# Attention in an AdaLN layer: key-block weights added by VectorE and GpSimd ahead of the product with ones

## The chip, the cores and the metric

One core of a Trainium2 chip runs the whole layer in one launch. The time is device microseconds of one execution; three executions of the kernel before took 2218.84, 2220.32 and 2224.95 us, a median of 2220.32 us. Lower is better.

## The reference

The input is four sequences of 1024 rows by 512 columns, all in float32. A modulated layer norm is followed by causal attention with 16 heads of 32 columns (its queries and keys are projected, rotated and normalised per head), a projection with a gate and a residual, and a gated feed-forward part. What the change touches is this line pair:

```
w = jax.nn.softmax(scores, axis=-1)          # causal, over the keys
a = jnp.einsum('bhqk,bhkd->bhqd', w, v)
```

The softmax's division is done at the end: the kernel computes, for every query, the sum of the exponentials times v and the sum of the exponentials alone, and divides the first by the second.

## The kernel before

The program has four stages: the projections to q, k and v (to about 367 us of the span), attention (to about 1010 us), the output projection, and the feed-forward part (from about 1140 us). The change is in the attention stage, `attention_stage`, alone.

**Groups and blocks.** The 16 x 4 head-and-sequence pairs are handled in 16 groups `n` of four heads `j`. In a group the queries come in four quarters `q` of 256, and the keys in slabs `g` of 256 (two key tiles of 128, `e` = 0 and 1). `BLOCKS` lists the ten causal (q, g) pairs: block 0 is (0,0), 1 (1,0), 2 (1,1), 3 (2,0), 4 (2,1), 5 (2,2), 6 (3,0), 7 (3,1), 8 (3,2), 9 (3,3). Blocks 0, 2, 5 and 9 are `DIAGONAL`; the other six are full ("full steps" in the change's short name).

**One block.** `shift` (TensorE) forms the transposed scores less the row maximum in PSUM, `exponent` (ScalarE) writes their exponentials for the four heads into `probT`, a ring of three buffers, `cut` (GpSimd) zeroes the triangle of diagonal blocks, and `weigh` (TensorE) runs twice: with `summing` false it multiplies with v, eight matmuls of 32 columns of weights; with `summing` true it multiplies with a matrix of ones, to get the sums. The four heads lie on different column groups of the array. Of a full block the sum may be taken after its two key tiles were added: `pair` adds `prob[:, :, 0:256]` and `prob[:, :, 256:512]` in two instructions of two heads each into one of the two buffers `pairs`, and then `weigh` needs only four matmuls with ones in place of eight. Before the change this is done for blocks 1, 3, 4, 6 and 8 (`PAIRED`): by VectorE for 3, 6 and 8 (`BY_VECTOR`), by GpSimd for 1 and 4. Block 7 is not paired.

**Other work in the same loop.** `score` (TensorE) forms the plain scores of a later group in two PSUM slots `psA`, `peak` (VectorE) takes their maxima (a reduce at L1104, a masked one at L1109); `gather` ends a group's maxima with four small operations, `turn_peaks` (TensorE, L1014) transposes them, `copy_peaks` (ScalarE) takes them out. `prepare` (TensorE, L993) transposes q or k of the next group into the same two slots, `widen` (ScalarE), `high` (GpSimd) and `low` (VectorE, L792) go on from there. Slots are handed on in the order of `turns`: whoever takes one waits (`slot_free`) until the user before the last has been read. `normalise` (GpSimd, L970) multiplies a finished group with the inverted sums, which come back by DMA (`wide_in`, L926).

**The order.** Every engine runs through the same written-out list of `STEPS`, and does its part for position k in program order. Within position k = 10 n + r, called turn r here: TensorE does two heads' `shift`, the `score` items of block position r, two heads' `shift`, `weigh` with v, `prepare` if r is 1 or 3, `turn_peaks` if r is 0, and `weigh` with ones. The shifts belong to block r - 2 of an earlier group, the two `weigh` to block r - 3 (both modulo 10). VectorE does `pair` for block r - 3 first, then the `peak` items, then `gather` in turn 9, then `low` in turns 2 and 4. GpSimd does `normalise` in turn 0, `cut` or `pair` for block r - 2, and `high` in turns 1 and 3. So block 4 is exponentiated and added by GpSimd in turn 6 and multiplied in turn 7; block 7 is multiplied in turn 0, and VectorE's pair of block 8 lies in turn 1. SyncE's queue lays the stacks of the next group in turns 4 to 7 (from the end of `low`), and issues `wide_in` in turn 8 and the peaks in turn 0.

Of the kernel before, what the change touches and what calls it, by code (L numbers as in the profile page):

```python
# [24 lines left out]
ALU = mybir.AluOpType  # L25
# [3 lines left out]
P = 128  # L29
# [4 lines left out]
HD = DM // H  # L34
# [629 lines left out]
W = HALF * P  # L664
QW = 2 * P
# [5 lines left out]
PROBS = 3  # L671
# [3 lines left out]
ITEMS = [(p, pieces) for p in range(2) for pieces in PIECES]  # L675
BLOCKS = [(q, g) for q in range(NQ) for g in range(q + 1)]
DIAGONAL = [w for w, (q, g) in enumerate(BLOCKS) if g == q]
PAIRED = [w for w, (q, g) in enumerate(BLOCKS) if g != q and w != len(BLOCKS) - 3]
BY_VECTOR = PAIRED[1::2] + PAIRED[4:]
NI, NW = len(ITEMS), len(BLOCKS)  # L680
SINGLE = (2, 4)
SHIFT_LAG = NW + 2
assert NI == 2 * NW - len(SINGLE)


def paired_index(n, w):

    return len(PAIRED) * n + PAIRED.index(w)


class Attention:

    def __init__(self, nc, args, scratch, sems):
        self.args, self.scratch = args, scratch

        def sem(name):
            return sems.enter_context(nc.semaphore(name))

        early, spot = placer(nc, BASE)
        self.ident = early("b_ident", [P, P])  # L700
# [12 lines left out]
        self.halves = early("b_halves", [P, 4, C], F32R)  # L713
        self.setup_at = spot[0]
        stack0 = early("b_stack0", [P, 2, 4, C], F32R)
        assert spot[0] <= BASE + EARLY_BYTES
        rest, spot = placer(nc, BASE + EARLY_BYTES)
        self.masked = rest("b_masked", [P, 2, 2, 2, P])
        self.probT = rest("b_probT", [P, PROBS, 4, W])
        self.pairs = rest("b_pairs", [P, 2, 4, QW])  # L720
        self.v = rest("b_v", [P, 2, TB, P])
        self.acc = rest("b_acc", [P, 2, 2, C])
        self.few = rest("b_few", [P, 2, C // HD])
        self.stacks = [stack0] + [rest(f"b_stack{n}", [P, 2, 4, C], F32R) for n in (1, 2)]
        assert spot[0] <= nc.sbuf_usable_end

        names = ("mask_in ln_ready whole consts ones_in qk_in v_in turned hi_done lo_done scored maxed peaks_ready "
                 "peaks_turned peaks_copied peaks_in shifted expd cut paired paired_v weighed summed taken sums_out few_in inverted few_out "
                 "wide_in scaled ended early_turned early_whole").split()
        self.s = {n: sem("b_" + n) for n in names}  # L730
        self.stack_in = [sem(f"b_stack_in{j}") for j in range(4)]
        self.stored = sem("b_stored")
# [70 lines left out]
def attention_stage(nc, args, scratch, a, before, block):  # L803
# [3 lines left out]
    pairs = a.pairs  # L807
# [57 lines left out]
    with ExitStack() as ctx:  # L865
# [81 lines left out]
        def _(pool):  # L947
# [4 lines left out]
                                   pattern=[[0, 4], [0, 2], [1, P]], channel_multiplier=-1).then_inc(s["cut"], 1)  # L952

            def pair(n, w):
                at = paired_index(n, w)
                if at >= 2:
                    before = NW * ((at - 2) // len(PAIRED)) + PAIRED[(at - 2) % len(PAIRED)]
                    pool.wait_ge(s["summed"], before + 1)
                for x in range(2):
                    heads = slice(2 * x, 2 * x + 2)  # L960
                    pool.wait_ge(s["expd"], 4 * (NW * n + w) + 2 * x + 2)
                    prob = probT[:, (NW * n + w) % PROBS, heads]
                    pool.tensor_tensor(pairs[:, at % 2, heads], prob[:, :, 0:QW], prob[:, :, QW:W], ALU.add).then_inc(s["paired"], 1)

            def normalise(n):
                pool.wait_ge(s["wide_in"], 64 * n + 64)
# [6 lines left out]
            for k in STEPS:  # L973
                n, w = unit(k)
# [10 lines left out]
        def _(pe):  # L985
# [51 lines left out]
            def weigh(n, w, summing):  # L1037
                q, g = BLOCKS[w]
                if not summing:
# [6 lines left out]
                    if g == 0:  # L1046
                        at_least(pe, s["taken"], NQ * n + q)
                out = psOL[:, 1 if summing else 0]
                if summing and w in PAIRED:
                    at = paired_index(n, w)  # L1050
                    for j in range(4):
                        if j % 2 == 0:
                            mine = [x for x in PAIRED if (x in BY_VECTOR) == (w in BY_VECTOR)]
                            count = 2 * (len(mine) * n + mine.index(w))
                            pe.wait_ge(s["paired_v" if w in BY_VECTOR else "paired"], count + j // 2 + 1)
                        mm = pe.matmul(out[j * HD:(j + 1) * HD], ones[:], pairs[:, at % 2, j],
                                       start=False, stop=False, skip_group_check=True)
                    mm.then_inc(s["summed"], 1)
                    return
# [29 lines left out]
        def _(dve):  # L1089
# [34 lines left out]
                dve.tensor_tensor(peaks[:, 4 * TB:8 * TB].bitcast(F32R), least[:], hi, ALU.subtract).then_inc(s["peaks_ready"], 1)  # L1124

            def pair(n, w):
                at = paired_index(n, w)
                if at >= 2:
                    before = NW * ((at - 2) // len(PAIRED)) + PAIRED[(at - 2) % len(PAIRED)]
                    dve.wait_ge(s["summed"], before + 1)  # L1130
                for x in range(2):
                    heads = slice(2 * x, 2 * x + 2)
                    dve.wait_ge(s["expd"], 4 * (NW * n + w) + 2 * x + 2)
                    prob = probT[:, (NW * n + w) % PROBS, heads]
                    dve.tensor_tensor(pairs[:, at % 2, heads], prob[:, :, 0:QW], prob[:, :, QW:W], ALU.add).then_inc(s["paired_v"], 1)

            def finish(q):
                n = NG - 1
# [30 lines left out]
        def _(act):  # L1169
# [8 lines left out]
            def exponent(n, w, j):  # L1178
                i = 4 * (NW * n + w) + j
                act.wait_ge(s["shifted"], i + 1)  # L1180
                if i == 0:
                    all_stored(act)
                if j == 0:
                    at_least(act, s["summed"], NW * n + w - 2)
                    at_least(act, s["weighed"], NW * n + w - 2)
                width = W - P if w in DIAGONAL else W
                act.activation(probT[:, (NW * n + w) % PROBS, j, 0:width], psB[:, i % BANKS, 0:width], ACT.Exp).then_inc(s["expd"], 1)  # L1187

# [3 lines left out]
                act.activation(peak_rows[:], slot("peaks", n)[0:8 * TB, 0, 0:P], ACT.Copy).then_inc(s["peaks_copied"], 1)  # L1192

            def take(n, q):
                act.wait_ge(s["summed"], NW * n + DIAGONAL[q] + 1)
                at_least(act, s["scaled"], n - 1)
                at_least(act, stored, 16 * (n - 1))
                act.activation(acc[:, :, n % 2, q * QW:(q + 1) * QW], psOL[:], ACT.Copy).then_inc(s["taken"], 1)
# [513 lines left out]
```

## Time and profile before

| | us |
|---|---|
| median of three executions | 2220.32 |
| the profiled execution | 2220.4 |
| its span, first to last instruction | 2218.7 |
| TensorE busy in the span | 2127.0 |
| VectorE busy | 1153.6 |
| ScalarE busy | 844.9 |
| GpSimd busy | 811.0 |

The profile shows one execution. A line of a timeline gives the start in us from the span's start, the time to the end of the last of its instructions, the engine, the line of the kernel, the operation, the tiles out<-in with their shapes, and how many instructions were merged into it; in square brackets, the idle time of the engine before it and who ended it. A float32 matmul leaves two records, so four matmuls appear as x8. PE is TensorE, DVE VectorE, ACT ScalarE, POOL GpSimd, SPq the queue of SyncE.

### The profile page before, as it was taken

To read this page: it belongs to the slowest core of one execution; us is meant where nothing else is said; L and a number is where in the kernel's file an instruction comes from. 1 tells how busy PE (TensorE), PEld (TensorE's weight loads), DVE (VectorE), ACT (ScalarE), POOL (GpSimd) and SP (SyncE) were. 2 spreads that over 40 slices of the span, in tenths; PEclk is the share of its full clock that TensorE was granted. 3 is DMA by queue.
4 is the path that set the end of the run, shared out by engine and by line. 5 is a ranking of instruction groups with operands and counts; after the bars stand their busy time and mean duration, and the time that the engine had idled before them with its cause. 6 is when DMAs were issued, how large, how long until landed. Compare 5 with 4: busy or idle time off the path is not lost. (4 is left out here: it accounts for less than half of the span.)

```text
span 2218.7 us, 35247 instructions
## 1 busy us (share of the span) xinstructions
PE 2127.0 (96%) x13416; PEld 1666.8 (75%) x13416; DVE 1153.6 (52%) x2713; ACT 844.9 (38%) x1671; POOL 811.0 (37%) x639
## 2 busy tenths in 40 slices
PE   5999997899999999996979999999999999999998
PEld 3778885677777777764758888888888888888887
DVE  4788897778878788855963222221222122222212
ACT  4455552366666666664761111111111111111111
POOL 1667776143444434344107522222222222222221
PEclk8999998699999999998989999999999999999999
DMA  6223353657576666616863311121212112121111
GB/s 205 101 100 118 112 164 119 158 122 172 143 167 152 158 159 152 143 51 198 298 239 119 100 67 34 48 77 57 67 53 72 34 53 71 53 71 57 51 30 57
DMA packets 178058, 244.14 MB, mean 110 GB/s; under 512 B 21517, under 2 KB 100493, under 8 KB 177897
## 3 DMA queue, kind: packets, MB, share of 16 engines
q1 hardware_dynamic: 175624, 235.66, 37.3%
q0 software_dynamic: 1216, 3.16, 0.5%
q10 hardware_dynamic: 1056, 3.15, 0.4%
q8 instruction: 104, 1.70, 0.3%
q14 instruction: 58, 0.47, 0.1%
HBM read 131.69 MB, written 59.26 MB: 86 GB/s over the span
## 5 line engine op out<-in xcount | busy, mean ns | idle before, releaser
L1571 DVE TENSOR_TENSOR f_gu<-f_psU,f_silu 128x512 f32<-128x512 f32 x128 | 88.5, 691 | 704.4 <-PE f_psU L1641 704.4
L1187 ACT ACTIVATE b_probT<-b_psB 128x512 f32<-128x512 f32 (+1 forms) x640 | 315.3, 555 | 140.4 <-PE b_psB L1033 140.3
L1527 POOL TENSOR_SCALAR f_wd_hi<-f_wd 128x512 fp32r<-128x512 f32 x128 | 84.9, 663 | 719.8 <-PE f_psD L1624 719.8
L1104 DVE TENSOR_REDUCE b_top<-b_psA 128x2 f32<-128x1024 f32 (+2 forms) x320 | 284.2, 900 | 79.1 <-PE b_psA L1006 78.9
L1547 ACT ACTIVATE f_silu<-f_psG 128x512 f32<-128x512 f32 x128 | 76.6, 598 | 504.9 <-PE f_psG L1641 504.9
L1033 PEld LDWEIGHTS b_psB<-b_stack 98*128 98x128 f32 x1280 | 184.6, 191 | 72.7 <-issue 38.4
L1033 PE MATMUL b_psB<-b_stack 98*128 98x256 f32 (+1 forms) x1280 | 219.2, 292 | 6.0 <-ACT b_probT L1187 3.7
L1542 ACT ACTIVATE f_gu_hi<-f_gu 128x512 fp32r<-128x512 f32 x128 | 80.9, 632 | 364.5 <-DVE f_gu L1571 364.5
L1639 PE MATMUL f_psG<-f_hT_hi,w_hi 128*128 128x512 f32 x512 | 200.3, 391 | 12.2 <-DVE f_hT_lo L1565 12.2
L1640 PE MATMUL f_psG<-f_hT_hi,w_lo 128*128 128x512 f32 x512 | 200.0, 391 | 0.0
L1641 PE MATMUL f_psG<-f_hT_lo,w_hi 128*128 128x512 f32 x512 | 200.0, 391 | 0.0
L1639 PE MATMUL f_psU<-f_hT_hi,w_hi 128*128 128x512 f32 x512 | 199.3, 389 | 0.0
L1640 PE MATMUL f_psU<-f_hT_hi,w_lo 128*128 128x512 f32 x512 | 199.3, 389 | 0.0
L1623 PE MATMUL f_psD<-f_wd_lo,f_gu_hi 128*128 128x512 f32 x512 | 199.3, 389 | 0.0
L1622 PE MATMUL f_psD<-f_wd_hi,f_gu_hi 128*128 128x512 f32 x512 | 199.3, 389 | 0.0
L1624 PE MATMUL f_psD<-f_wd_hi,f_gu_lo 128*128 128x512 f32 x512 | 199.3, 389 | 0.0
L1641 PE MATMUL f_psU<-f_hT_lo,w_hi 128*128 128x512 f32 x512 | 199.3, 389 | 0.0
L1006 PE MATMUL b_psA<-b_stack 96*128 96x512 f32 (+3 forms) x768 | 183.9, 369 | 10.0 <-DVE b_top L1104 5.1
L1529 POOL TENSOR_TENSOR f_wd_lo<-f_wd,f_wd_hi 128x512 fp32r<-128x512 f32 x128 | 167.8, 1311 | 10.6
L1065 PE MATMUL b_psOL<-b_probT,b_v 128*32 128x256 f32 (+1 forms) x2560 | 158.3, 365 | 0.4 <-POOL b_probT L951 0.4
L632 PE MATMUL a_psQ<-wqkv_hi,hT_hi 128*128 128x512 f32 x384 | 156.1, 406 | 0.0
L633 PE MATMUL a_psQ<-wqkv_lo,hT_hi 128*128 128x512 f32 x384 | 153.0, 398 | 0.0
(175 smaller groups left out, 3971.1 us busy)
## 6 DMA issues: line engine op xcount, KB each, us to landing
b_stack<-b_halves SPq DMA_DIRECT2D x192, 256.0 KB, 4.8
f_wd<-in_wd_t SPq DMA_DIRECT2D x128, 256.0 KB, 2.7
qkv_d<-a_t SPq DMA_DIRECT2D x32, 512.0 KB, 2.7
b_land<-qkv_d SPq DMA_DIRECT2D x32, 512.0 KB, 5.0
a_x<-in_x SPq DMA_DIRECT2D x32, 256.0 KB, 3.5
qkv_d<-a_v SPq DMA_DIRECT2D x32, 256.0 KB, 3.2
b_v<-qkv_d SPq DMA_DIRECT2D x16, 512.0 KB, 6.9
att_d<-b_acc SPq DMA_DIRECT2D x16, 512.0 KB, 3.0
```

Of the source, the lines that this page charges most:

```text
L1006: mm = pe.matmul(out[:, h, col:col + (hi - lo) * P], stacks[n % BUFS][0:ROWS, 1, j, t * P:(t + 1) * P], stacks[n % BUFS][0:ROWS, 0, j, lo ...
L1033: mm = pe.matmul(psB[:, i % BANKS, e * QW:e * QW + (2 * q + 2 - first) * P], stacks[n % BUFS][0:NR, 0, j, kb * P:(kb + 1) * P], stacks[n % ...
L1065: mm = pe.matmul(out[rows, (first - 2 * q) * P:QW], ones[:] if summing else v[:, n % 2, kb, rows], probT[:, (NW * n + w) % PROBS, j, e * Q ...
L1104: last = dve.tensor_reduce(into, tile[:, :, col:col + whole_blocks * P], AX.X, ALU.max, negate=True)
L1187: act.activation(probT[:, (NW * n + w) % PROBS, j, 0:width], psB[:, i % BANKS, 0:width], ACT.Exp).then_inc(s["expd"], 1)
L1529: pool.tensor_tensor(wd_lo[:, u % 2], wd[:, u % 2], wd_hi[:, u % 2].bitcast(F32), ALU.subtract).then_inc(s["wd_lo"], 1)
L1622: pe.matmul(out_t, gu_hi[:, u % 2, cols], wd_hi[:, u % 2], start=first, stop=False)
L1623: pe.matmul(out_t, gu_hi[:, u % 2, cols], wd_lo[:, u % 2], start=False, stop=False)
L1624: mm = pe.matmul(out_t, gu_lo[:, u % 2, cols], wd_hi[:, u % 2], start=False, stop=end)
L1639: pe.matmul(out_c, w_hi[:, m, k, cols], hi, start=(k == 0), stop=False)
L1640: pe.matmul(out_c, w_lo[:, m, k, cols], hi, start=False, stop=False)
L1641: mm = pe.matmul(out_c, w_hi[:, m, k, cols], lo, start=False, stop=(k == KC - 1))
```

## The change

All six full blocks are paired. VectorE adds blocks 3, 6, 7 and 8, GpSimd blocks 1 and 4. Block 3's sum gets no product of its own: after GpSimd has added block 4's halves into buffer 0, it adds block 3's sum (buffer 1, written by VectorE) to it in two more instructions, and the product with ones of block 4 covers both. `pairs` has three buffers, with a fixed place for each block (`PLACE`). The waits follow: the counts of `summed` (now nine a group), `paired` and `paired_v` come from three helper functions, and `exponent`, which reuses block w - 3's buffer, waits for VectorE's pair of block 3 where it waited for its product.

```diff
-PAIRED = [w for w, (q, g) in enumerate(BLOCKS) if g != q and w != len(BLOCKS) - 3]
-BY_VECTOR = PAIRED[1::2] + PAIRED[4:]
+PAIRED = [w for w, (q, g) in enumerate(BLOCKS) if g != q]
+BY_VECTOR = [3, 6, 7, 8]
+MERGED = {4: 3}
+PLACE = {1: 0, 3: 1, 4: 0, 6: 1, 7: 2, 8: 0}
+SUMMING = [w for w in range(len(BLOCKS)) if w not in MERGED.values()]
...
-        self.pairs = rest("b_pairs", [P, 2, 4, QW])
+        self.pairs = rest("b_pairs", [P, 3, 4, QW])
...
             def pair(n, w):
-                at = paired_index(n, w)
-                if at >= 2:
-                    before = NW * ((at - 2) // len(PAIRED)) + PAIRED[(at - 2) % len(PAIRED)]
-                    pool.wait_ge(s["summed"], before + 1)
+                before = {1: (n - 1, 8), 4: (n, 1)}[w]
+                at_least(pool, s["summed"], summed_by(*before) if before[0] >= 0 else 0)
+                prob = probT[:, (NW * n + w) % PROBS]
                 for x in range(2):
                     heads = slice(2 * x, 2 * x + 2)
                     pool.wait_ge(s["expd"], 4 * (NW * n + w) + 2 * x + 2)
-                    prob = probT[:, (NW * n + w) % PROBS, heads]
-                    pool.tensor_tensor(pairs[:, at % 2, heads], prob[:, :, 0:QW], prob[:, :, QW:W], ALU.add).then_inc(s["paired"], 1)
+                    pool.tensor_tensor(pairs[:, 0, heads], prob[:, heads, 0:QW], prob[:, heads, QW:W], ALU.add).then_inc(s["paired"], 1)
+                if w in MERGED:
+                    pool.wait_ge(s["paired_v"], paired_v_by(n, MERGED[w]))
+                    for x in range(2):
+                        heads = slice(2 * x, 2 * x + 2)
+                        pool.wait_ge(s["paired"], paired_by(n, w) - 3 + x)
+                        pool.tensor_tensor(pairs[:, 0, heads], pairs[:, 0, heads], pairs[:, 1, heads], ALU.add).then_inc(s["paired"], 1)
...
+                if summing and w in MERGED.values():
+                    return
                 if summing and w in PAIRED:
...
+                        if j % 2 == 0 and w in BY_VECTOR:
+                            pe.wait_ge(s["paired_v"], paired_v_by(n, w) - 1 + j // 2)
+                        elif j % 2 == 0:
+                            pe.wait_ge(s["paired"], paired_by(n, w) - 1 + j // 2)
+                        mm = pe.matmul(out[j * HD:(j + 1) * HD], ones[:], pairs[:, PLACE[w], j],
...
                 if j == 0:
-                    at_least(act, s["summed"], NW * n + w - 2)
                     at_least(act, s["weighed"], NW * n + w - 2)
+                    if NW * n + w >= PROBS:
+                        last = divmod(NW * n + w - PROBS, NW)
+                        if last[1] in MERGED.values():
+                            act.wait_ge(s["paired_v"], paired_v_by(*last))
+                        else:
+                            act.wait_ge(s["summed"], summed_by(*last))
```

VectorE's `pair` writes to `PLACE[w]`; for block 6 it waits for GpSimd's merge of block 4 (which reads buffer 1), for 3, 7 and 8 for products of the buffer's last user.

## Rows read from the trace of the kernel before

**Rows 1.** By stretch: us, busy PE PEld DVE ACT POOL, PEclk, DMA share, GB/s.

```profile
585.00:623.00 38.00, 37.86 (x427) 27.54 (x426) 30.53 (x98) 24.18 (x47) 15.89 (x12) 1.00 0.67 158
...
1060.00:1070.00 10.00, 7.69 (x34) 5.65 (x34) 9.53 (x20) 6.41 (x18) 3.74 (x2) 1.00 0.80 279
```

**Rows 2.** Timeline of TensorE (PE), turns 6 and 7 of one group.

```profile
618.01 0.74 PE L1033 MATMUL b_psB<-b_stack 98*128 98x256 f32 x4
...
620.10 1.07 PE L1065 MATMUL b_psOL<-b_probT,b_v 128*32 128x256 f32 x16
620.99 0.61 PE L1056 MATMUL b_psOL<-b_pairs,b_ones 128*32 128x256 f32 x8
...
624.51 0.61 PE L1056 MATMUL b_psOL<-b_pairs,b_ones 128*32 128x256 f32 x8
625.05 0.74 PE L1033 MATMUL b_psB<-b_stack 98*128 98x256 f32 x4
```

**Rows 3.** Timeline of TensorE (PE), turns 0 and 1.

```profile
634.23 1.07 PE L1065 MATMUL b_psOL<-b_probT,b_v 128*32 128x256 f32 x16
635.23 0.33 PE L1014 MATMUL b_psA<-b_ident,b_peaks 128*128 128x128 f32 x1
635.49 1.07 PE L1065 MATMUL b_psOL<-b_probT,b_ones 128*32 128x256 f32 x16
636.49 0.67 PE L1033 MATMUL b_psB<-b_stack 98*128 98x256 f32 x4
...
639.60 1.09 PE L993 MATMUL b_psA<-b_ident,b_land 128*128 128x128 f32 x8
```

**Rows 4.** Timeline of GpSimd (POOL), turns 6 and 7.

```profile
619.87 2.55 POOL L963 TENSOR_TENSOR b_pairs<-b_probT 128x512 f32<-128x512 f32 x2 [4.16 <-ACT b_probT L1187]
624.45 1.10 POOL L951 TENSOR_SCALAR_AFFINE_SELECT b_probT<-b_probT 128x1024 f32<-128x1024 f32 x1 [2.03 <-ACT b_probT L1187]
```

**Rows 5.** Timeline of VectorE (DVE), turns 0 and 1.

```profile
633.66 2.35 DVE L1104 TENSOR_REDUCE b_top<-b_psA 128x2 f32<-128x1024 f32 x2
635.92 1.28 DVE L1135 TENSOR_TENSOR b_pairs<-b_probT 128x512 f32<-128x512 f32 x2
637.72 0.42 DVE L1104 TENSOR_REDUCE b_top<-b_psA 128x2 f32<-128x256 f32 x1 [0.52 <-PE b_psA L1006]
...
639.24 0.28 DVE L1109 CUSTOM_DVE_ANT_0 b_masked<-b_psA,b_mask 128x128 f32<-128x128 f32 x1
```

**Rows 6.** Timelines of VectorE and TensorE, first transposition of peaks.

```profile
401.79 2.35 DVE L1104 TENSOR_REDUCE b_top<-b_psA 128x2 f32<-128x1024 f32 x2
...
403.15 0.45 PE L1014 MATMUL b_psA<-b_ident,b_peaks 128*128 128x128 f32 x1 [0.90 <-DVE b_top L1104]
```

**Rows 7.** Normalising multiplies, L970, from 480 to 945 us: ns min/median/max.

```profile
L970 POOL TENSOR_TENSOR b_acc<-b_acc x26: 1268/1282/1463, 485.6 to 941.7; 128x512 f32<-128x512 f32 x26
```

**Rows 8.** Timelines: the largest and smallest distance of L970 from the pair.

```profile
560.11 1.28 DVE L1135 TENSOR_TENSOR b_pairs<-b_probT 128x512 f32<-128x512 f32 x2
...
562.84 2.51 POOL L970 TENSOR_TENSOR b_acc<-b_acc 128x512 f32<-128x512 f32 x2 [13.11 <-DMA b_acc<-sums_d]
...
711.71 1.28 DVE L1135 TENSOR_TENSOR b_pairs<-b_probT 128x512 f32<-128x512 f32 x2
...
712.66 2.71 POOL L970 TENSOR_TENSOR b_acc<-b_acc 128x512 f32<-128x512 f32 x2 [11.35 <-DMA b_acc<-sums_d]
```

**Rows 9.** Timelines: VectorE and GpSimd at once, feed-forward part.

```profile
1311.48 4.00 DVE L1591 TENSOR_TENSOR f_land<-f_land,f_scaled 128x512 f32<-128x512 f32 x4
1312.26 0.99 POOL L1527 TENSOR_SCALAR f_wd_hi<-f_wd 128x512 fp32r<-128x512 f32 x1 [6.16 <-PE f_psD L1624]
1313.33 1.61 POOL L1529 TENSOR_TENSOR f_wd_lo<-f_wd,f_wd_hi 128x512 fp32r<-128x512 f32 x1
```

**Rows 10.** Timelines of GpSimd and TensorE, last group, turns 6 and 7.

```profile
991.01 2.71 POOL L963 TENSOR_TENSOR b_pairs<-b_probT 128x512 f32<-128x512 f32 x2 [4.46 <-ACT b_probT L1187]
...
994.58 0.61 PE L1056 MATMUL b_psOL<-b_pairs,b_ones 128*32 128x256 f32 x8
```

More of the change, by code:

```diff
@@ L683, with summed_by, paired_by, paired_v_by @@
 assert NI == 2 * NW - len(SINGLE)
-def paired_index(n, w):
-    return len(PAIRED) * n + PAIRED.index(w)
+def summed_by(n, w):
+    return len(SUMMING) * n + sum(1 for x in SUMMING if x <= w)
+def paired_by(n, w):
+    return sum(4 if x in MERGED else 2 for x in PAIRED if x not in BY_VECTOR) * n + sum(4 if x in MERGED else 2 for x in PAIRED if x not in BY_VECTOR and x <= w)
+def paired_v_by(n, w):
+    return 2 * (len(BY_VECTOR) * n + sum(1 for x in BY_VECTOR if x <= w))
 class Attention:
@@ L1048, in weigh @@
                 out = psOL[:, 1 if summing else 0]
+                if summing and w in MERGED.values():
+                    return
                 if summing and w in PAIRED:
-                    at = paired_index(n, w)
                     for j in range(4):
[L1052 to L1056, printed above, removed]
+                        if j % 2 == 0 and w in BY_VECTOR:
[3 more added lines that the diff above has]
+                        mm = pe.matmul(out[j * HD:(j + 1) * HD], ones[:], pairs[:, PLACE[w], j],
                                        start=False, stop=False, skip_group_check=True)
@@ L1126, in pair @@
             def pair(n, w):
[L1127 to L1130, printed above, removed]
+                if w == 6:
+                    dve.wait_ge(s["paired"], paired_by(n, 4))
+                else:
+                    before = {3: (n - 1, 6), 7: (n - 1, 7), 8: (n, 4)}[w]
+                    at_least(dve, s["summed"], summed_by(*before) if before[0] >= 0 else 0)
+                prob = probT[:, (NW * n + w) % PROBS]
                 for x in range(2):
@@ L1133, in pair @@
                     dve.wait_ge(s["expd"], 4 * (NW * n + w) + 2 * x + 2)
-                    prob = probT[:, (NW * n + w) % PROBS, heads]
-                    dve.tensor_tensor(pairs[:, at % 2, heads], prob[:, :, 0:QW], prob[:, :, QW:W], ALU.add).then_inc(s["paired_v"], 1)
+                    dve.tensor_tensor(pairs[:, PLACE[w], heads], prob[:, heads, 0:QW], prob[:, heads, QW:W], ALU.add).then_inc(s["paired_v"], 1)
             def finish(q):
@@ L1183, in exponent @@
                 if j == 0:
-                    at_least(act, s["summed"], NW * n + w - 2)
                     at_least(act, s["weighed"], NW * n + w - 2)
+                    if NW * n + w >= PROBS:
+                        last = divmod(NW * n + w - PROBS, NW)
+                        if last[1] in MERGED.values():
+                            act.wait_ge(s["paired_v"], paired_v_by(*last))
+                        else:
+                            act.wait_ge(s["summed"], summed_by(*last))
                 width = W - P if w in DIAGONAL else W
@@ L1194, in take @@
             def take(n, q):
-                act.wait_ge(s["summed"], NW * n + DIAGONAL[q] + 1)
+                act.wait_ge(s["summed"], summed_by(n, DIAGONAL[q]))
                 at_least(act, s["scaled"], n - 1)
```

## The prediction, made before the changed kernel ran

> **What bounds the kernel now.** I read the page's engine table first (in the section on the profile), then a table by stretch, then the timelines of one head group engine by engine. TensorE is busy 2127.0 of 2218.7 us, and in the attention stretch 37.86 of every 38 us at full clock; VectorE has 30.53 us of work there and GpSimd 15.89 [rows 1]. So the attention loop is bound by TensorE, one head group after another every 37.9 us (the pair of block 8 starts at 560.11 and four groups later at 711.71) [rows 8], and fewer matmuls can pay. But VectorE's work is not even: from turn 8 to turn 0 it runs without a gap, which the timeline has to show and the busy share hides. I use "block w" for the key block w of a group and "turn r" for the loop position k mod 10; turn r holds the exponents of block r-2, the products of block r-3 and the scores of a later group. The instance read is the group between 618 and 642 us; the others repeat it.
>
> **What TensorE saves.** In turn 6 the product of block 3's sum goes (eight records, four matmuls). It starts at 620.99 and, as block 4's does (624.51 to 625.05), holds TensorE for 0.54, so turn 7 begins at 621.53 [rows 2]. Without it the product with v, which starts at 620.10, is followed by the next turn's first matmul, and the same step without a product of sums behind it, in turn 0, takes 634.23 to 635.23 = 1.00 instead of 0.89 [rows 2, 3]. So the turn ends at 618.01 + 2.09 + 1.00 = 621.10, a gain of 0.43. In turn 0 block 7's product with ones shrinks from 16 records, 635.49 to 636.49 = 1.00, to the eight-record form, 0.54: a gain of 0.46. With no new wait, 16 x (0.43 + 0.46) = 14.2 us.
>
> **Turns 6 and 7: GpSimd's merge.** Today GpSimd adds block 4's halves from 619.87 to 622.42, two adds back to back, released by ScalarE's exponents, which follow turn 6's shifts [rows 4]. TensorE takes them at 624.51 [rows 2], so 2.1 us are spare; with turn 6 shorter by 0.43 it would want them at 624.08. The change puts two more adds behind them. No row shows an add into the same tile of this shape but L970's (median 1282 ns) [rows 7], and the two existing adds are 1.28 each; I take 1.28. Bounds: 0 (were it overlapped) and 1.46, the slowest L970. The merges end at 622.42 + 2.56 = 624.98. TensorE's heads 2 and 3 wait for the second; with 0.13 us from an engine's end to TensorE's start (of the two reduces that began at 401.79 and took 2.35, the first ends at about 403.02, its 1.23 overlapping the next by 0.1; the matmul that waits for it starts at 403.15) [rows 6] they start at 625.11. The four heads run side by side in two passes, so the last two alone still take the 0.54. Turn 8 begins at 625.65 instead of 625.05: **+0.60 a group**, although a product was removed; the 0.43 is in this number. ScalarE's last exponents of block 4 are done by 621.15, when GpSimd's second add runs; turn 7, which needs them, would start at 621.10, so 0.1 can be lost there, hidden behind the wait that follows. Behind the merges GpSimd has the cut of block 5 (1.10): 624.98 to 626.08 [rows 4], wanted by TensorE behind turn 8's shifts and scores, which took 2.09 in turn 6: 627.74; nothing. It applies to the 15 groups whose turn 7 still carries scores: 15 x 0.60 = 9.0 us.
>
> **Turn 0: VectorE's added pair.** VectorE's pair for block 7 is first in turn 0, behind the small peak operations and ahead of the two reduces that now start at 633.66. A pair takes 1.28, and the next instruction starts 0.09 before the last ends (the reduces end at 636.01, the pair starts at 635.92), so it costs 1.20 [rows 5]. The first reduce frees the PSUM slot that the transposition of the peaks takes: it ends at 634.89 now, TensorE wants it at 635.23, so the slack is 0.21 behind 0.13 of signalling. With the pair: 636.09, transposition at 636.22, its 0.26, the short product 0.54, turn 1 at 637.02 instead of 636.49: **+0.53**, the 0.46 being in it [rows 3, 5]. I take 0.52. The chain starts with TensorE's scores of turn 8 (VectorE waits there), so it is not shortened by the wait in turn 7, and the two add up. It counts where scores remain and a block 7 exists: 14 x 0.52 = 7.3 us. In turn 1 the pair of block 8 now runs 637.12 to 638.32, where TensorE's next scores are ready at about 638.24; so it costs nothing by itself. TensorE's transpositions of turn 1 need the slot of that turn's first score: VectorE is through with it when it turns to the second at 639.24, TensorE starts at 639.60 [rows 3, 5], 0.23 spare behind the signal, and 0.15 once VectorE is 0.60 and TensorE 0.53 later.
>
> **Turn 1: who holds the port.** GpSimd's normalising multiplies (two, 2.51 together) wait for a DMA [rows 8] whose issue is tied to turn 4 (SyncE's queue runs on from there), not to turn 1. They start after the start of block 8's pair by 1.24, 2.59, 2.73, 2.34, 1.75, 1.25, 0.95, 1.53, 1.69, 2.08, 2.73, 1.64 and 1.43 us in the 13 groups where scores surround them (the extremes in [rows 8]). Both sides read two SBUF tensors. Where such instructions meet, the rows show that they take turns, each for its whole length: four VectorE adds, 0.6 apart when alone, took 4.00 us with two GpSimd operations in between, and these took 0.99 and 1.61 where the same add of GpSimd takes 1.28 elsewhere [rows 9]. The second column of starts (1312.26, 1313.33) fits one in, one out. After the change the pair of block 8 starts 0.60 + 1.20 = 1.80 later against the DMA. So 8 of the 13 would start before the pair (on the average 0.36 before): the pair waits for the first and lets the second in between, 2.51 - 0.36 = 2.15 us later. Two fall into its first half (1.26), three behind it (0). The pair's delay reaches TensorE at turn 1's transpositions, less the 0.15: 8 x 2.00 + 2 x 1.11 = 18.2 us. Bounds: 0 (if the DMA moves with the turn) and 13 x 2.36 = 31 us.
>
> "SBUF — State Buffer" of the Trainium skill (section "SBUF: two separate sides") calls this pair of ports "an exclusive lock", held for the whole instruction by whoever starts first. The adds of 4.00 us [rows 9] agree. By that rule the 18.2 us above stand; without a lock the total would lack them. It speaks against giving VectorE and GpSimd more adds in SBUF side by side.
>
> **The tail.** With no scores, turns are short. Block 7 of the last but one group saves 0.4. In the last group the four adds run 991.01 to 993.72 and on to 996.28, where TensorE takes the product at 994.58 today [rows 10]: the next turn starts at 996.28 + 0.13 + 0.54 = 996.95 instead of 995.12, +1.8, less 0.46 for its block 7. Together +1.0.
>
> **Sum.** 9.0 + 7.3 + 18.2 + 1.0 = 35.5 us. The profiled span is 2218.7 and the profiled execution 2220.4, equal to the runs' median of 2220.32 within 0.1. So 2220.4 + 35.5 = 2255.9, taken as **2256.0 us**, 1.6% slower. The three exponent waits that change their semaphore, the third pairs buffer and the other pair waits look back to products that ended a turn or more before: nothing.
>
> **The rivals.** *A. The two new waits, no port collisions.* For: the 13 starts are set by a DMA, and it may land elsewhere. Against: its issue precedes turn 0. Time: 2220.4 + 17.3 = 2237.7. *B. One of the two waits fails to appear.* Only GpSimd's: 9.0 - 16 x 0.46 + 1.8 = +3.4, 2223.8; only VectorE's: 7.3 - 16 x 0.43 = +0.4, 2220.8. Against: the shorts are 1.0 us each, by durations that hardly vary. *C. Faster: TensorE stays the bound in both turns.* It decides if the two merges together need less than 624.08 - 0.13 - 622.42 = 1.53 us and VectorE has found time for the pair before 633.66. For: 37.86 of 38 us busy [rows 1]. Against: the first is 1 us short of rows that all say 1.28. Time: 2220.4 - 14.2 = 2206.2. *D. Worse: the waits lower TensorE's clock.* Waits of 1 to 2 us, up to three a group, might bring 1.2 GHz for stretches. Were it low for a tenth of the loop's 570 us (15 groups), half of that, 28 us, would be lost on top: 2284. Against: from 1060 to 1070 us TensorE was busy 7.69 of 10 us and the granted clock stayed 1.00 [rows 1]. "TensorE: Matmul & The Clock Gate" of the Trainium skill (section "A second HAM failure mode") tells of a kernel whose frequent short idle times made the clock swing; the row speaks against it here. *E. The change doesn't do what it says*, for instance block 3's product left in: both gains in TensorE are countable, and the early return in the diff is plain; 2%.
>
> **Chances.** Forecast (2245 to 2266) 0.53; A 0.20; B 0.09; C 0.07; D and other additions above 2266 0.09; E 0.02. A difference of 0.3%, 6.7 us, is what can be told from none. C is faster: 0.08 with a share of E. B is the same: 0.10. The rest slower: 0.82. The range reaches from 2228 (A with merges at their cheap bound) to 2266 (a collision in nearly every group) and holds the forecast, A and a little of the rest, about 0.78.
>
> **What would show it.** L1056's successor: 16 x 4 products fewer for block 3, 16 x 4 more for block 7 in place of eight with ones; TensorE waiting for GpSimd's pairs in turn 7 with about 1 us a group, 15 times; for VectorE's reduce before the transposition of the peaks with about 1 us, 14 times; VectorE pairs of over 1.7 us in turn 1 about eight to ten times, and TensorE's transpositions waiting behind them. A group would take about 39 us without a collision and 41 with one. If TensorE's busy share stays at 99% in the loop, C holds. If the pair of block 8 keeps 0.68 us everywhere, A holds. If merges take 0.7, the first wait was wrong.

## The result and the profile after

The changed kernel took 2252.88 us (median of four executions, 2249.03 to 2258.52) against 2219.58 us before: 1.0142 times as long, 95% interval 1.0127 to 1.0157. The forecast was 2256.0. The profiled execution has a span of 2250.3 us, 31.6 more than before. The first line below is the page's busy time by engine, the other two a table by stretch with the columns of [rows 1].

```profile
PE 2128.3 (95%) x13160; PEld 1660.4 (74%) x13160; DVE 1181.7 (53%) x2745; ACT 845.6 (38%) x1671; POOL 857.7 (38%) x671
```

```profile
560.00:602.00 42.00, 40.00 (x439) 28.43 (x439) 34.77 (x106) 25.32 (x50) 19.06 (x14) 1.00 0.65 152
640.00:682.00 42.00, 38.87 (x434) 27.45 (x422) 34.83 (x101) 24.76 (x49) 19.25 (x14) 1.00 0.63 145
```

TensorE has 256 records fewer, 16 x 16, so the change does what it says; yet TensorE now stands idle for 2.0 and 3.1 of 42 us where it stood idle for 0.14 of 38 [rows 1], at an unchanged clock. The waits of the attention loop, 433 to 1045 us (engine, line, who is waited for: us in total, times, the longest), name three places:

```profile
PE b_psA L1010 <- DVE b_corner L1127: 14.4, 11, 2.0
PE b_psA L1031 <- DVE b_top L1122: 12.5, 14, 0.9
PEld b_psOL L1074 <- POOL b_pairs L980: 10.5, 17, 1.4
```

L1010 is turn 1's transposition of q or k, L1031 turn 0's transposition of the peaks, L1074 the product of pairs in turn 7. Before, the same list has nothing over 0.4 us for any of the three. The third shows in the weight load (PEld), because the last two heads' matmuls wait in it. Turns 6 to 8 of a group, TensorE and GpSimd:

```profile
626.42 0.74 PE L1050 MATMUL b_psB<-b_stack 98*128 98x256 f32 x4
...
631.84 1.07 PE L1083 MATMUL b_psOL<-b_probT,b_v 128*32 128x256 f32 x16
632.72 1.26 PE L1074 MATMUL b_psOL<-b_pairs,b_ones 128*32 128x256 f32 x8
633.91 0.74 PE L1050 MATMUL b_psB<-b_stack 98*128 98x256 f32 x4
```

```profile
628.28 2.54 POOL L974 TENSOR_TENSOR b_pairs<-b_probT 128x512 f32<-128x512 f32 x2 [4.13 <-ACT b_probT L1211]
630.79 2.51 POOL L980 TENSOR_TENSOR b_pairs<-b_pairs 128x512 f32<-128x512 f32 x2
633.26 1.09 POOL L964 TENSOR_SCALAR_AFFINE_SELECT b_probT<-b_probT 128x1024 f32<-128x1024 f32 x1
```

The product that took 0.61 in [rows 2] takes 1.26: its four matmuls start in two lots, the second behind GpSimd's last merge (633.30). Turns 6 and 7 together take 7.49 us, 0.45 more than in [rows 2]. Turns 0 and 1 of the same group, all three engines:

```profile
642.52 1.29 DVE L1154 TENSOR_TENSOR b_pairs<-b_probT 128x512 f32<-128x512 f32 x2
643.73 2.35 DVE L1122 TENSOR_REDUCE b_top<-b_psA 128x2 f32<-128x1024 f32 x2
```

```profile
645.09 0.30 PE L1031 MATMUL b_psA<-b_ident,b_peaks 128*128 128x128 f32 x1 [0.92 <-DVE b_top L1122]
645.32 0.64 PE L1074 MATMUL b_psOL<-b_pairs,b_ones 128*32 128x256 f32 x8
645.89 0.67 PE L1050 MATMUL b_psB<-b_stack 98*128 98x256 f32 x4
645.92 2.97 POOL L987 TENSOR_TENSOR b_acc<-b_acc 128x512 f32<-128x512 f32 x2 [11.57 <-DMA b_acc<-sums_d]
645.99 3.46 DVE L1154 TENSOR_TENSOR b_pairs<-b_probT 128x512 f32<-128x512 f32 x2
...
651.10 1.07 PE L1010 MATMUL b_psA<-b_ident,b_land 128*128 128x128 f32 x8 [2.02 <-DVE b_corner L1127]
```

The pair of block 7 stands ahead of the two maxima, and the transposition waits 0.92 for the first of them. Then GpSimd's multiply starts 0.07 ahead of block 8's pair, and the pair takes 3.46 instead of 1.28 [rows 5]; what stands behind it is late, and TensorE waits 2.02.

From one transposition of the peaks to the next a group takes 38.84 us where nothing collides in turn 1 (37.90 before, the mean of the 13 in the middle; +0.94), 39.84 with a short collision, and 40.4 to 40.9 with a long one. The first of these transpositions came 0.20 us later than before, the last 27.88, attention's last matmul 28.95, the first feed-forward matmul 29.74.

### The profile page after: what moved, and what is told of

It reads as the page before. It is cut to its first block and busy times, and to the rows that moved or that the text cites. A ratio compares the mean times of both kernels' runs of the same rounds, so it can differ in the third digit from the quotient of the medians.

```text
span 2250.3 us, 34830 instructions
## 1 busy us (share of the span) xinstructions
PE 2128.3 (95%) x13160; PEld 1660.4 (74%) x13160; DVE 1181.7 (53%) x2745; ACT 845.6 (38%) x1671; POOL 857.7 (38%) x671
## 5 line engine op out<-in xcount | busy, mean ns | idle before, releaser
L1023 PE MATMUL b_psA<-b_stack 96*128 96x512 f32 (+3 forms) x768 | 186.9, 371 | 10.0 <-DVE b_top L1122 5.1
```

The costliest lines, as they stand in the source:

```text
L1023: mm = pe.matmul(out[:, h, col:col + (hi - lo) * P], stacks[n % BUFS][0:ROWS, 1, j, t * P:(t + 1) * P], stacks[n % BUFS][0:ROWS, 0, j, lo ...
```

## The experiments

Each edit is against the changed kernel unless it says otherwise. The theory: two waits (turn 7 and turn 0) and a port collision in turn 1. The main rival: one of these causes, or TensorE's rhythm in general, accounts for all.

**Without the merge.** Block 3's sum is multiplied with ones on its own again.

```diff
-MERGED = {4: 3}
+MERGED = {}
-                    dve.wait_ge(s["paired"], paired_by(n, 4))
+                    at_least(dve, s["summed"], summed_by(n, 3))
```

> The changed kernel, but block 3 keeps its own product with ones and GpSimd merges nothing (block 7 is still paired by VectorE). Theory (three separate waits): the wait in turn 7 is gone, so turn 6 and 7 are as before the change; turn 0 keeps its wait (14 x 0.54 = 7.6 us); block 8's pair now starts 1.20 instead of 1.65 us later against the normalising multiplies, so that about 1 of 13 starts before it (1.9 us) and 7 in its first half (0.95 each), 8.6 us; the last two groups give back 0.9. 7.6 + 8.6 - 0.9 = 15.3: 2235 us, TensorE waiting for GpSimd's pairs nowhere. Rival (the loss is the load of two more pairs of adds on VectorE and GpSimd, in proportion to their number): half of 33 us is left, 2236 us as well, but then e2 gives 2236 too. Rival (GpSimd's merge is the whole cause): 2212 us, since TensorE keeps the 0.46 us of block 7.

Measured: 2235.83 us, ratio 1.0064 (1.0040 to 1.0089). Waits in the loop:

```profile
PE b_psA L1031 <- DVE b_top L1122: 12.5, 14, 0.9
PE b_psA L1010 <- DVE b_corner L1127: 6.5, 6, 1.8
```

TensorE no longer waits for GpSimd's pairs; turn 0's wait is untouched to the tenth. An uncollided group takes 38.42 us (+0.52), a collided one 39.42. So the pair of block 7 costs 0.52 by itself.

**Without the pair of block 7.**

```diff
-PAIRED = [w for w, (q, g) in enumerate(BLOCKS) if g != q]
-BY_VECTOR = [3, 6, 7, 8]
+PAIRED = [w for w, (q, g) in enumerate(BLOCKS) if g != q and w != 7]
+BY_VECTOR = [3, 6, 8]
```

> The changed kernel, but block 7 is not paired (eight matmuls with ones, as before); GpSimd still merges block 3 into block 4. Theory: turn 7's wait stays, 15 x 0.45 = 6.8 us, and 1.8 in the last group; turn 0 is as before the change; block 8's pair starts only 0.45 us later against the multiplies, so about 1 of 13 meets its first half, 1.0. Together 9.6: 2229 us, with next to no long pairs. Rival (load in proportion to the adds): 2236 us. Rival (VectorE's added pair is the whole cause): 2213 us.

Measured: 2228.68 us, ratio 1.0035 (1.0022 to 1.0047).

```profile
PEld b_psOL L1074 <- POOL b_pairs L980: 10.4, 17, 1.4
```

Only this wait is left, and every group takes 38.34 us (+0.44). In the 13 groups no pair of block 8 is held up: it comes early again. 0.44 + 0.52 = 0.96, against 0.94 with both: the two waits add up, and the collisions come on top.

**The multiplies moved behind the cut.** In the changed kernel and, as a control, in the kernel before, GpSimd's `normalise` goes from turn 0 to turn 1, behind the cut of block 9, so that it can't meet block 8's pair.

```diff
-                if w == 0 and 0 <= n - 3 < NG - 1:
-                    normalise(n - 3)
                 if cut_at(k):
                     cut(*cut_at(k))
+                if w == 1 and 0 <= n - 3 < NG - 1:
+                    normalise(n - 3)
```

> The changed kernel with GpSimd's normalising multiplies moved from turn 0 to turn 1, behind the cut of block 9, when VectorE's pair of block 8 is over. Nothing else. Theory (meeting at the shared port costs 11 waits of 0.95 to 2.0 us in turn 1, 14.4 us of idle time, 15 us in all): 2238 us, all pairs of block 8 back at 1.28 us, waits in turns 7 and 0 unchanged (0.45 and 0.54 us a group). Rival (the long pairs only fill time in which TensorE would wait for VectorE's maxima or for something else anyway): 2253 us.

> The kernel before the change with the same move of the normalising multiplies: the control of e3. Theory: in the kernel before they collide only once at the end of a pair, so the move is worth nothing and costs nothing: 2219.6 us, within 0.2%. Rival (the new place is itself better or worse, through the cut, GpSimd's rounding of whole or the store): another time, and e3 has to be read against it.

Measured: 2238.82 us, ratio 1.0077 (1.0060 to 1.0094), with a period of 39.26 us in 12 of the 13 groups; and for the kernel before with the same move 2227.87 us, ratio 1.0027 (1.0016 to 1.0038), 38.33 in 12 of 13. The control was expected to cost nothing and cost 0.43 a group. Its timeline, and then the same place in the kernel before:

```profile
641.64 2.52 POOL L970 TENSOR_TENSOR b_acc<-b_acc 128x512 f32<-128x512 f32 x2
...
644.12 1.05 POOL L787 TENSOR_SCALAR b_halves<-b_whole 128x1024 fp32r<-128x1024 f32 x1
645.12 1.11 POOL L951 TENSOR_SCALAR_AFFINE_SELECT b_probT<-b_probT 128x1024 f32<-128x1024 f32 x1
645.21 2.10 DVE L792 TENSOR_TENSOR b_halves<-b_whole,b_halves 128x1024 fp32r<-128x1024 f32 x1 [0.40 <-POOL b_halves L787]
```

```profile
643.56 1.21 DVE L792 TENSOR_TENSOR b_halves<-b_whole,b_halves 128x1024 fp32r<-128x1024 f32 x1
643.59 2.14 POOL L951 TENSOR_SCALAR_AFFINE_SELECT b_probT<-b_probT 128x1024 f32<-128x1024 f32 x1 [0.46 <-ACT b_probT L1187]
```

The multiplies hold up GpSimd's `high` (L787), and VectorE's `low` (L792) waits for that: it starts 2.86 us into turn 2 instead of 2.37. There it has lost its place: before, it started 0.03 ahead of the cut of block 0 and the cut paid for the meeting (2.14 instead of 1.10), now the cut starts 0.09 ahead and `low` pays (2.10 instead of 1.21). It ends 1.38 later in the turn, and turn 3 is 0.43 longer. Of the 1.38 some 0.95 were to spare, so the later start of 0.49 alone would have cost nothing; by this estimate the control's loss is a port collision too. Without collisions in turn 1 and with the control's 0.43 the changed kernel's group should take 38.84 + 0.43 = 39.27, and it takes 39.26. So the collisions of turn 1 are worth the difference of the medians, 2252.88 - 2238.82 = 14.1, and up to 12 x 0.43 = 5.2 more that the moved multiplies cost: 14 to 19 us. In the changed kernel's own trace they are 14.9 (13 periods' sum less 13 x 38.84).

**Block 8's pair between the two maxima of turn 1.** A second way past the collision.

```diff
+                between = score_at(k) and vector_pair_at(k) and vector_pair_at(k)[1] == 8
-                if vector_pair_at(k):
+                if vector_pair_at(k) and not between:
                     pair(*vector_pair_at(k))
...
                         peak(n, item)
+                        if between and x == 0:
+                            pair(*vector_pair_at(k))
```

> The changed kernel, with one thing moved: in turn 1 VectorE adds block 8's halves between the two maxima of that turn instead of ahead of both. GpSimd's multiplies (2.5 us) start with the turn and are over, or nearly, when the pair starts about 2.8 us into it, so the two meet at the port in two groups at most; the pair is still there before TensorE's product with ones wants it (about 4.1 us into the turn). Theory (the port cost of turn 1 is all that lies between the uncollided period of 38.83 us and the others, 11 waits with 15.2 us in all): every group takes 38.8 us, no transposition of turn 1 waits over 0.3 us, and the time falls to 2252.9 - 15.2 = 2237.7 us, which is rival A of the prediction. Rival (the added work of VectorE is what makes turn 1 late, wherever the port stands, or the second maximum, now 1.2 us later, is waited for instead): waits of 0.5 to 1.2 us stay in turn 1 or 2 of all groups, 2245 us or more.

Measured: 2254.41 us, ratio 1.0146 (1.0130 to 1.0161): nothing gained. All groups take 40.1 us, with no multiply in the pair's way. The waits in the loop, and VectorE and GpSimd in turns 1 and 2:

```profile
PEld b_psOL L1074 <- DVE b_pairs L1154: 11.4, 15, 1.4
PEld b_psA L1023 <- DVE b_corner L1127: 7.3, 27, 0.4
```

```profile
650.71 2.19 DVE L1154 TENSOR_TENSOR b_pairs<-b_probT 128x512 f32<-128x512 f32 x2
650.89 1.46 POOL L964 TENSOR_SCALAR_AFFINE_SELECT b_probT<-b_probT 128x1024 f32<-128x1024 f32 x1 [0.20 <-ACT b_probT L1214]
...
656.29 1.10 POOL L964 TENSOR_SCALAR_AFFINE_SELECT b_probT<-b_probT 128x1024 f32<-128x1024 f32 x1 [1.68 <-ACT b_probT L1214]
656.31 2.16 DVE L805 TENSOR_TENSOR b_halves<-b_whole,b_halves 128x1024 fp32r<-128x1024 f32 x1
```

The pair now starts 0.18 us ahead of the cut of block 9 and takes 2.19; TensorE's product with ones waits for it, and turn 1 takes 5.55 us instead of the uncollided 4.71. At its own 1.28 us the pair would end at 651.99, ahead of the product's first half (652.10), so it is the meeting with the cut and not the later place that costs TensorE here. One turn on, TensorE's scores wait for the maxima that now stand behind the pair (L1023 in the list), and turn 2 is 0.34 longer; an estimate from these rows leaves about 0.3 of it without any collision, since VectorE would be through with them 0.91 earlier and TensorE want their slot 0.84 earlier. Last, `low` and the cut of block 0 start 0.02 apart: in 10 of the 13 groups `low` takes 2.16 instead of 1.22, and turn 3 is 0.08 longer in just these. The collision with the multiplies is gone; a collision with a cut in every group (0.84) and the later second maxima (0.3) have taken its place. The forecast for this run was right on the multiplies and wrong on what is late next.

**Other divisions of the adds.** All three leave GpSimd's merge out and give it blocks 1, 4, 6 and 7, VectorE 3 and 8. Then VectorE alone merges: nothing (`MERGED` is empty), block 3's sum into 4's (`{4: 3}`), or besides 6's into 7's (`{4: 3, 7: 6}`).

```diff
-BY_VECTOR = [3, 6, 7, 8]
-MERGED = {4: 3}
-PLACE = {1: 0, 3: 1, 4: 0, 6: 1, 7: 2, 8: 0}
+BY_VECTOR = [3, 8]
+MERGED = {}
+PLACE = {1: 0, 3: 1, 4: 2, 6: 0, 7: 1, 8: 2}
```

> All six full blocks paired, none merged: GpSimd adds blocks 1, 4, 6 and 7 (it is idle from turn 8 to the normalising multiplies), VectorE 3 and 8; six products of sums a group. Theory: block 7's sums are ready by 633.1 us in the clock of the group read from the kernel before, taken at 635.5, so TensorE keeps the whole 0.46 us a group; VectorE loses block 6's pair in turn 9, so the transposition of the peaks waits nowhere; block 8's pair runs before the multiplies. 2219.6 - 16 x 0.46 = 2212.2 us, period of a group 37.44 us. Rival (pairing block 7 costs what the change cost, whoever adds, because of load or of the port): 2220 us or more.

> As e5, and block 3's sum is merged into block 4's, by VectorE at the start of turn 7 where the change has GpSimd do it; block 3 has no product. Theory: VectorE adds the first half when GpSimd lets go of the port (622.4 in the clock of the kernel before) and the second until 623.65; TensorE wants it at 624.08. So the wait of 0.45 us becomes a gain of 0.43 a group: 2212.2 - 6.9 = 2205.3 us, period 37.0 us. Its two adds delay VectorE's maxima of turn 7 by about 1.2 us, for which turns 7 and 8 have 1.5 idle. Rival (a merge costs TensorE a wait wherever it is, since the sum of block 4 is final too late): 2212 us or more.

> As e6, and block 6's sum is merged into block 7's by VectorE in turn 0, between the two items of maxima, so that the slot of the peaks is free first; four products of sums a group. Theory: the merge ends at about 634.9 in the clock of the kernel before, TensorE wants it at 635.06, and the second item's maxima are over at 636.1 where TensorE's next scores want the slot: at best another 16 x 0.43 = 6.9 us, 2198.4 us, period 36.55; each of the margins is 0.1 or less, so that up to half of it may be lost (2202). Rival (VectorE is the bound in turn 0 again): 2206 us or more, TensorE waiting for VectorE's maxima in turns 0 and 1.

Measured: 2216.03 us, ratio 0.9977 (0.9968 to 0.9986), faster than both kernels; 2219.27, ratio 0.9988 (0.9979 to 0.9997); and 2246.84, ratio 1.0111 (1.0095 to 1.0126).

Without a merge a group takes 37.47 us, 0.43 less than before, close to the 0.46 expected of block 7's shorter product. The executions lie between 2212.3 and 2221.0; the profiled one took 2220.1, and in it 4.0 us go at one place near the loop's end (its last period is 38.66 us, 34.66 before), where a DMA landed late:

```profile
937.00 2.51 POOL L984 TENSOR_TENSOR b_acc<-b_acc 128x512 f32<-128x512 f32 x2 [6.34 <-DMA b_acc<-sums_d]
...
939.47 2.15 POOL L967 TENSOR_SCALAR_AFFINE_SELECT b_probT<-b_probT 128x1024 f32<-128x1024 f32 x2
940.62 1.50 PE L1080 MATMUL b_psOL<-b_probT,b_v 128*32 128x256 f32 x16 [1.69 <-POOL b_probT L967]
```

The matmuls behind that wait take 1.50 instead of 1.07: from 940 to 945 us the mean granted clock is 0.66, which is 3.4 us at the lower of its two levels.

With VectorE's merge of block 3 the group takes 37.56 where 37.0 was expected. Turn 6 gives its 0.43, and turns 7 and 8 take it back, since VectorE's merge (655.53, 1.39 us) puts the maxima behind it late: `PEld b_psA L1020 <- DVE b_top` waits 15 times. With both merges TensorE waits for VectorE's adds and maxima in all places at once, 38.4 to 42.0 us a group:

```profile
PEld b_psOL L1071 <- DVE b_pairs L1156: 16.3, 34, 1.4
PE b_psA L1007 <- DVE b_corner L1124: 8.9, 6, 2.1
```

It was the worst forecast of all (2198.4 expected): it had counted VectorE's adds at their length and forgotten that block 8's pair would meet the multiplies again.

**Two more adds by GpSimd.** To price the wait in turn 7: block 4's sum is added to itself before the merge (so it is counted twice in the result).

```diff
+                    for x in range(2):
+                        heads = slice(2 * x, 2 * x + 2)
+                        pool.wait_ge(s["paired"], paired_by(n, w) - 5 + x)
+                        pool.tensor_tensor(pairs[:, 0, heads], pairs[:, 0, heads], pairs[:, 0, heads], ALU.add).then_inc(s["paired"], 1)
```

> The changed kernel with two more adds on GpSimd between block 4's own and the merge (block 4's sum is added to itself, so that this part of the sum is counted twice). Theory (turn 8 starts when GpSimd's last add has ended): 2.52 us later in each of 15 groups, 37.8 us, and 2.5 in the last group; but block 8's pair then starts another 2.5 us later against the normalising multiplies, so that most of them are over before it (3 to 5 of 13 still meet it), and 8 to 12 us of the meetings' 15 go. 2252.9 + 40.3 - 10 = 2283 us, TensorE's wait for GpSimd's merge about 3.4 us a group. Rival (GpSimd's adds cost by load, 33 us for 64 adds of both engines): 2270 us. Rival (the wait in turn 7 is hidden behind something else): about 2253 us.

Measured: 2287.36 us, ratio 1.0306 (1.0276 to 1.0336), 34.5 more than the changed kernel. An uncollided group takes 40.8 us, 1.96 more; two groups of 46.5 and 43.9 us stand out, with TensorE's granted clock at 0.50 for nearly 7 us twice between 683 and 707 us. GpSimd's two more adds and the merges in one group, and then TensorE, where the wait that hid in the load now shows on both lots:

```profile
636.32 2.04 POOL L979 TENSOR_TENSOR b_pairs<-b_pairs 128x512 f32<-128x512 f32 x2
638.31 2.48 POOL L984 TENSOR_TENSOR b_pairs<-b_pairs 128x512 f32<-128x512 f32 x2
```

```profile
639.62 0.63 PE L1078 MATMUL b_psOL<-b_pairs,b_ones 128*32 128x256 f32 x4 [1.18 <-POOL b_pairs L984]
640.85 0.63 PE L1078 MATMUL b_psOL<-b_pairs,b_ones 128*32 128x256 f32 x4 [0.60 <-POOL b_pairs L984]
```

The two adds of a tile to itself (L979) are shorter than the 1.26 us of the merges behind them (L984): 1.04 us each, in all 32. So GpSimd's six adds take 6.97 us where four took 5.02, 1.95 more, and turn 7 takes 6.35 where it took 4.40, 1.95 more. All that GpSimd adds in turn 7 is on the path; the expectation had the right path and 2.52 us for these adds.

**The DMA one turn earlier.** In the fastest version (no merge, GpSimd 1, 4, 6, 7) SyncE issues the DMA of the inverted sums in turn 7.

```diff
-                if 0 <= n - 2 < NG - 1 and w in (3, 4, 6, 8):
-                    {3: sums_out, 4: few_in, 6: few_out, 8: wide_in}[w](n - 2)
+                if 0 <= n - 2 < NG - 1 and w in (3, 4, 6, 7):
+                    {3: sums_out, 4: few_in, 6: few_out, 7: wide_in}[w](n - 2)
```

> The kernel in which GpSimd adds blocks 1, 4, 6 and 7, VectorE 3 and 8, and no sum is merged (2216.0 us), with the DMA of the inverted sums issued one turn earlier by SyncE, ahead of the last quarter of the stacks. Theory: the 4 us that it lost once, where GpSimd's multiplies waited 6.3 us for that DMA and its cut behind them came late, go: 2216.0 - 3.8 = 2212.2 us, with a period of 37.47 us throughout. Rival (that loss was one late landing of DMAs in general and the last quarter of the stacks, now behind, comes late instead): 2216 or more, with TensorE waiting for the stacks or the loss elsewhere.

Measured: 2255.25 us, ratio 1.0155 (1.0141 to 1.0169), against an expected gain. The wait for the DMA is gone, and a wait of 1.78 us before the transposition of the peaks is there 13 times (23.0 us in all). VectorE, GpSimd and TensorE around one:

```profile
641.38 2.54 POOL L984 TENSOR_TENSOR b_acc<-b_acc 128x512 f32<-128x512 f32 x2
641.50 1.22 DVE L1134 SCALAR_TENSOR_TENSOR b_least<-b_corner,b_least 128x32 f32<-128x32 f32 x1
...
642.76 1.20 DVE L1137 CAST b_peaks<-b_least 128x32 fp32r<-128x32 f32 x1
643.99 0.19 DVE L1139 TENSOR_TENSOR b_peaks<-b_least,b_peaks 128x32 fp32r<-128x32 f32 x1
...
645.46 0.38 PE L1028 MATMUL b_psA<-b_ident,b_peaks 128*128 128x128 f32 x1 [1.78 <-DVE b_top L1119]
```

The multiplies now start with `gather`. Two of its operations, 0.19 and 0.18 us long alone, take 1.22 and 1.20 us, as long as one multiply: each ends only when a multiply has ended, and one multiply is let in between them. The two maxima behind them are 2 us late. The rest of the loss is TensorE's clock, in two groups side by side:

```profile
563.90:603.20 39.30, 37.37 (x417) 27.17 (x418) 31.77 (x96) 24.20 (x47) 21.01 (x16) 1.00 0.63 150
603.20:645.50 42.30, 40.37 (x418) 29.24 (x418) 31.88 (x96) 24.32 (x47) 21.04 (x16) 0.92 0.58 140
```

The same matmuls in the same order take 39.3 us in one and 42.3 in the other. Behind 4 of the 13 waits the clock fell to its lower level for nearly 7 us (3.1 us lost each time), behind a fifth for half as long. These 14 us and the 23 us of the waits, less 6 us up to the end of the first group and in the last (where the 4.0 us of the late DMA are gone), make attention end 31 us later.

## Why the prediction was right, point by point

- **TensorE's saving** of 0.43 in turn 6 and 0.46 in turn 0: right. The first shows with VectorE's merge of block 3 (turn 6 takes 3.10 us instead of 3.53), the second in the version without a merge (37.90 to 37.47, so 0.43).
- **Turn 7**: the right wait, mis-sized, +0.60 predicted and +0.45 measured. The four adds took 5.02 us rather than 5.11 (2.54 and 2.51, the second starting before the first's end), and turn 8 began 0.61 behind the last merge where the sum had 0.13 + 0.54 = 0.67: the weight load started 0.05 behind GpSimd's end, not 0.13. The 0.13 was read from a matmul that waits with its weights loaded, and in turn 7 it is the load that waits. The run with two more adds shows that nothing covers this wait.
- **Turn 0**: +0.53 predicted, +0.52 measured, by the run without the merge in which it stands alone.
- **How often**: the sum counted 15 and 14 groups at full price. The 13 periods in the middle pay it; the first and the last are only 0.21 and 0.22 longer. The two waits came to 27.88 - 0.20 - 14.9, about 12.7 us instead of 16.3: of the 3.6 too much some 2.3 lie in the size, nearly all of it turn 7's, and 1.3 in the count.
- **Turn 1**: the collision was there and decided the result. Predicted: 8 long, 2 short, 3 none, 18.2 us. Measured: 5 multiplies started ahead of the pair (by 0.07 to 0.59; the pair 1.66 to 2.18 longer), 6 in its first half or 0.03 ahead (1.10 longer), 2 met nothing; 11 waits of 14.35 us, and with the slack they ate, 14.9 us. The mean distance from pair to multiply shrank from 1.84 us to 0.13, by 1.71 (1.80 predicted): the DMA did stay where it was. That 11 met where the sum had 10 was near; the split into long and short failed in the spread about that mean, with twelve of the 13 within 0.65 us of a tie, which the sum had shifted one by one from another execution of the same DMAs. Of the 3.3 us too much about 1.5 come from that split and 1.8 from the price: a long one made turn 1 longer by 1.78 on the average (2.00 in the sum), a short one by 0.99 (1.11).
- **The tail**: +1.0 predicted, +1.07 measured. The last group's two lots wait for GpSimd:

```profile
1022.73 0.63 PE L1074 MATMUL b_psOL<-b_pairs,b_ones 128*32 128x256 f32 x4 [0.91 <-POOL b_pairs L980]
1023.95 0.63 PE L1074 MATMUL b_psOL<-b_pairs,b_ones 128*32 128x256 f32 x4 [0.59 <-POOL b_pairs L980]
```

- **Behind attention** the sum had nothing, and the span has 2.7 us (31.6 less 28.95). Of these 1.9 lie in the feed-forward part, 1053.8 us before and 1055.7 after. Its first ten us, of before and of after:

```profile
1164.90:1174.90 10.00, 9.40 (x32) 7.10 (x33) 5.47 (x5) 3.29 (x5) 8.14 (x6) 0.79 0.27 80
```

```profile
1194.60:1204.60 10.00, 9.35 (x23) 6.91 (x24) 4.80 (x3) 2.70 (x4) 8.25 (x6) 0.55 0.27 79
```

  The mean granted clock of the ten us is 0.24 lower: it came up to its upper level about 9.0 us into this part instead of 4.3. Nothing in the code differs there, and it isn't the change's doing: of the twelve profiled executions in this document, one of each kernel, six took 1053.7 to 1053.8 us from the first feed-forward matmul to the end (the kernel before, both halves of the change alone and three more) and six 1055.6 to 1055.9, among them the kernel before with nothing but its multiplies moved. From attention's end to that matmul the twelve differ by up to 3.2 us in the same way. So nothing ties these 2.7 us to the change, and they bring the profiled pair nearer to the forecast than the loop was.
- **Rivals.** A (no collision) is excluded by the pairs of 2.4 to 3.5 us, B and C by the waits that each single edit left standing, E by the count of records. The stated range alone would not have told A from the forecast, since it held A's 2237.7 too; the parts above do. D did not happen here: in no stretch of 5 us between 440 and 1000 is the granted clock under 0.98, in spite of a wait of 2.02. But it was no idle fear. In the version with the earlier DMA it fell behind waits of 1.78 us, and in the run without the merge behind two, of 1.79 and 1.48 us.

So 35.5 predicted against 31.7 between the two profiled executions and 33.3 between the medians: right by its mechanism, with 3.6 and 3.3 us too much in the waits and the collisions, 0.2 too little ahead of the loop, and 2.7 behind it that are luck.

## What to carry to other kernels

An engine that is busy four fifths of the time (VectorE here), or even two fifths (GpSimd), may have no room at all in the turn where you put the work: follow the turn's queue, instruction by instruction, to the PSUM slot that somebody waits for. Where VectorE and GpSimd both work in SBUF, an add moved in time must be placed against every SBUF operation of the other engine in that stretch, and each way out of one collision is to be read for the next: both ways tried here ran into the cut of a diagonal block. Of the two halves of this change the shorter product of block 7 pays (0.43 us a group) when GpSimd, which has the room, makes the sum. A merge paid in none of the four comparisons that isolate one: by GpSimd in the changed kernel and without block 7's pair, by VectorE of block 3 (37.56 us a group against 37.47) and of block 6.

## What the hardware showed that was not expected

- **Who goes first at a near tie.** A multiply that started 0.07 us ahead of the pair held it up for its whole length, one that started 0.03 ahead did not. A start alone doesn't tell, though: with block 8's pair between the maxima, cuts that started 0.02 ahead of `low` did hold it up. The case of 0.03, with the changed kernel's normalising multiply first and block 8's pair next:

```profile
606.16 3.54 POOL L987 TENSOR_TENSOR b_acc<-b_acc 128x512 f32<-128x512 f32 x2 [11.61 <-DMA b_acc<-sums_d]
606.19 2.37 DVE L1154 TENSOR_TENSOR b_pairs<-b_probT 128x512 f32<-128x512 f32 x2
```

  Here the multiplies pay 1.03 us (3.54 against 2.51) and the pair 1.09.
- **A collision costs the short instruction most.** Operations of 0.19 us took 1.2 us each beside multiplies of 1.27 in the version with the earlier DMA. "SBUF — State Buffer" of the Trainium skill (section "SBUF: two separate sides") has the port pair locked for the whole of an instruction by whoever started; the trace agrees, and adds that the two engines take turns instruction by instruction. So in these traces the price is one foreign instruction for each of one's own, whatever its size.
- **The clock after waits of 1.5 to 2.0 us.** It fell behind 4 or 5 of 13 waits of 1.78 us in one kernel, behind 1.79 and 1.48 in a second, behind 1.69 in a third, behind one of two waits of 2.15 in the version with both merges, and behind none of the 11 in turn 1 of the changed kernel (up to 2.02). "TensorE: Matmul & The Clock Gate" of the Trainium skill (section "A second HAM failure mode: psum-queue depth-cycling") tells of such a clock that swings with short idle times; the changed kernel's trace does not show it, that of the kernel with the earlier DMA does. What separates them stays open.
